# Cross-attention, MLP and a second attention over four batches: entries of the slot tables moved

## The reference

```
z = layer_norm(x, ln1_w, ln1_b)
q = z @ q_w + q_b;  k = ctx @ k_w + k_b;  v = ctx @ v_w + v_b        # 16 heads of 16
o = softmax(q k^T / 4) v                                            # per head
hidden = o @ cproj_w + cproj_b + x
y = gelu(layer_norm(hidden, ln2_w, ln2_b) @ fc_w + fc_b) @ proj_w + proj_b   # 1024 wide
h = hidden + y
# second attention, one head of width 256 over the same context
p = softmax((h @ w_q^T)(ctx @ w_k^T)^T / 16)
out = h + alpha * (p (ctx @ w_v^T)) @ w_o^T
```

## Time and profile before

| | |
|---|---|
| device time, median of 3 runs | 304.48 us (302.76 to 305.58) |
| the profiled execution | 301.47 us, span 299.7 us |
| busy, share of the span | PE 89%, PE weight loads 73%, DVE 70%, ACT 61%, POOL 29% |
| mean granted PE clock | 0.983 of full |
| chain that ended last, by engine | PE 57%, DVE 13%, ACT 9%, POOL 8%, DMA 5%, issue 5% |

### The profile page before, as it was taken

The page is one execution under the profiler, slowest core; times in us unless marked ns, Lnnn a source line. Parts: engine busy times, 40 slices in busy tenths (PEclk is TensorE's granted clock), DMA queues, the critical chain, the costliest instruction groups (busy, mean ns, idle before and its releaser), DMA issues.

```text
span 299.7 us, 5383 instructions
## 1 busy us (share of the span) xinstructions
PE 266.8 (89%) x2054; PEld 219.3 (73%) x2054; DVE 208.4 (70%) x369; ACT 182.8 (61%) x332; POOL 87.6 (29%) x106
## 2 busy tenths in 40 slices
PE   5966979998988998998979998989998999898995
PEld 4754857795666887776967886668876797678974
DVE  6846686577689689856598689654668665457763
ACT  3762666568584777865465959573647598336522
POOL 5360101102022267520031395400031274334000
PEclk9997699999999999999999999999999999999999
DMA  6059948611363330303340420203124000000001
GB/s 219 13 75 185 220 97 266 155 46 36 80 161 71 142 81 0 83 0 111 121 116 7 164 53 30 53 29 88 63 91 142 1 2 0 0 2 0 2 35 35
DMA packets 16424, 23.02 MB, mean 77 GB/s; under 512 B 2512, under 2 KB 9168, under 8 KB 16400
## 3 DMA queue, kind: packets, MB, share of 16 engines
q1 hardware_dynamic: 13088, 16.98, 22.8%
q10 hardware_dynamic: 3312, 5.71, 6.1%
HBM read 12.07 MB, written 1.05 MB: 44 GB/s over the span
## 4 chain that ended last, share of the span: by engine, by line
PE 57%; DVE 13%; ACT 9%; POOL 8%; DMA 5%; issue 5%; SPq 1%; ACTq 1%; POOLq 0%; DVEq 0%
PE work_ps L619 11%; PE om L703 8%; PE s L693 7%; PE s L667 7%; PE work_ps L623 5%; PE work_ps L606 4%; DVE neg_max L1437 4%; DMA q_stack<-qp_l 3%; POOL y_l L1801 2%; ACT probs L1114 2%; PE s L619 2%; POOL ft L1796 2%; PE om L682 2%; DMA vecs<-in_vectors_dram 2%; DVE cT_l L1401 1%
## 5 line engine op out<-in xcount | busy, mean ns | idle before, releaser
L1437 DVE TENSOR_REDUCE neg_max<-s 128x1 f32<-128x512 f32 x128 | 83.9, 684 | 25.8 <-PE s L667 25.3
L1114 ACT ACTIVATE probs<-s 128x512 f32<-128x512 f32 x128 | 75.5, 598 | 30.0 <-PE s L693 29.6
L693 PE MATMUL s<-q_stack,k_stack 128*128 128x256 f32 x256 | 56.5, 304 | 4.0 <-ACT probs L1114 2.1
L667 PE MATMUL s<-k_stack,q_stack 96*128 96x512 f32 x128 | 51.8, 436 | 7.1 <-DVE neg_max L1437 3.6
L693 PEld LDWEIGHTS s<-q_stack,k_stack 128*128 128x128 f32 x256 | 43.9, 197 | 10.9 <-ACT probs L1114 4.1
L667 PEld LDWEIGHTS s<-k_stack,q_stack 96*128 96x128 f32 x128 | 23.7, 198 | 17.8 <-DVE neg_max L1437 8.4
L1752 POOL CAST max_cols<-neg_max 128x8 fp32r<-128x8 f32 x16 | 5.8, 363 | 93.3 <-DVE neg_max L1437 93.3
L703 PE MATMUL om<-probs,vals 128*17 128x256 f32 x512 | 30.7, 380 | 0.0
L703 PEld LDWEIGHTS om<-probs,vals 128*17 128x17 f32 x512 | 13.4, 97 | 11.6 <-issue 0.2
L1106 ACT ACTIVATE q_stack<-om 8x1024 fp32r<-8x1024 f32 x16 | 16.3, 1019 | 7.6 <-PE om L682 7.3
L1128 ACT ACTIVATE y_h<-work_ps 128x512 fp32r<-128x512 f32 x12 | 7.2, 597 | 18.5 <-PE work_ps L623 17.0
(11 more groups left out here) (298 smaller groups left out, 675.0 us busy)
## 6 DMA issues: line engine op xcount, KB each, us to landing
k_stack<-kp_h SPq DMA_DIRECT2D x32, 128.0 KB
cx<-in_ctx_t_dram SPq DMA_DIRECT2D x4, 512.0 KB, 4.5
k_stack<-kp_l SPq DMA_DIRECT2D x16, 128.0 KB
q_stack<-qp_h SPq DMA_DIRECT2D x30, 64.0 KB
pcx<-in_ctx_dram ACTq DMA_DIRECT2D x3, 512.0 KB, 3.4
pT_raw<-in_ctx_t_dram ACTq DMA_DIRECT2D x3, 512.0 KB, 4.4
xz<-in_x_dram SPq DMA_DIRECT2D x5, 256.0 KB, 3.3
raw_late<-in_L_xattn_fc_w_dram SPq DMA_DIRECT2D x1, 1024.0 KB, 6.8
```

What stands on the lines that cost most here:

```text
L667: pe.matmul(s1[:, s1_bank(b, SLOTS * g + s), :], q_stack[0:ROW_MAX, hd, chunk(t)], k_stack[0:ROW_MAX, hd, :], start=True, stop=True).then_ ...
L693: mm = pe.matmul(s2[:, s2_bank(b, SLOTS * g + s), i * LQ:(i + 1) * LQ], k_stack[:, hd, chunk(k)], q_stack[:, hd, :], start=True, stop=True)
L1114: act.activation(probs[:, g % 2, s // 2, k:k + 2, :], s2[:, s2_bank(b, SLOTS * g + s), :].rearrange("p (k n) -> p k n", k=2), ACT.Exp).the ...
L1437: dve.tensor_reduce(neg_max[:, g % 2, s % 2, s // 2:s // 2 + 1], s1[:, s1_bank(b, SLOTS * g + s), :], AX.X, ALU.max, negate=True).then_inc ...
```

## The change

Numbers in the tables move; nothing else. The work and its amount are the same, the order on PE, DVE, ACT and POOL is not. SP's order is the same.

```diff
-POST_FIRST = (8, 11, 12, 13, 14, 15, 19, 25, 26, 31, 35)
+POST_FIRST = (7, 8, 13, 19, 20, 24, 25, 28, 30, 31, 32, 33, 34, 37)
-LN1_APPLY_AT = 8
-CT_AT = {7: 0, 8: 1}
-CT_LOW_AT = {8: 0, 9: 1}
-PRE_AT = {9: 0, 10: 1, 16: 2, 22: 3}
+LN1_APPLY_AT = 9
+CT_AT = {9: 0, 10: 1}
+CT_LOW_AT = {13: 0, 14: 1}
+PRE_AT = {9: 0, 11: 1, 17: 2, 22: 3}
...
-EARLY_AT = {11: 0, 14: 1, 16: 2, 24: 3}
+EARLY_AT = {11: 0, 13: 1, 16: 2, 29: 3}
```

More of the change, by code:

```diff
@@ L69 @@
 FIRST_ORDER = (U_ZT, U_K, U_Q, U_K + 1, U_V, U_V + 1)
-POST_FIRST = (8, 11, 12, 13, 14, 15, 19, 25, 26, 31, 35)
+POST_FIRST = (7, 8, 13, 19, 20, 24, 25, 28, 30, 31, 32, 33, 34, 37)
 LN1_AT = 7
-LN1_APPLY_AT = 8
-CT_AT = {7: 0, 8: 1}
-CT_LOW_AT = {8: 0, 9: 1}
-PRE_AT = {9: 0, 10: 1, 16: 2, 22: 3}
+LN1_APPLY_AT = 9
+CT_AT = {9: 0, 10: 1}
+CT_LOW_AT = {13: 0, 14: 1}
+PRE_AT = {9: 0, 11: 1, 17: 2, 22: 3}
 V_AT = {36: 0, 38: 1}
-POST_AT = {7: 'OT', 8: 'NT', 9: 'CP', 11: 'ZT', 14: 'F0', 15: 'F1', 18: 'F2', 19: 'F3', 20: 'PJ0', 21: 'PJ1',
+POST_AT = {7: 'OT', 8: 'NT', 9: 'CP', 11: 'ZT', 14: 'F0', 16: 'F1', 18: 'F2', 19: 'F3', 20: 'PJ0', 21: 'PJ1',
            22: 'CT0', 24: 'PJ2', 25: 'CT1', 26: 'PJ3', 27: 'CX', 28: 'HT', 29: 'G', 30: 'S0', 31: 'S1', 33: 'PT0',
            34: 'PT1', 35: 'PC', 36: 'DL'}
-EARLY_AT = {11: 0, 14: 1, 16: 2, 24: 3}
+EARLY_AT = {11: 0, 13: 1, 16: 2, 29: 3}
 LATE_AT = {7: 'OT', 9: 'NT', 11: 'CP', 14: 'ZT', 16: 'F0', 20: 'F1', 22: 'F2', 23: 'PJ0', 25: 'F3', 26: 'PJ1',
-           27: 'CT0', 29: 'PJ2', 30: 'CT1', 32: 'PJ3', 34: 'CX', 37: 'HT', 38: 'G', 41: 'S0', 43: 'S1', 46: 'PT0',
-           47: 'PT1', 49: 'PC', 51: 'DL'}
+           28: 'CT0', 29: 'PJ2', 31: 'CT1', 32: 'PJ3', 33: 'CX', 37: 'HT', 38: 'G', 43: 'S0', 44: 'S1', 46: 'PT0',
+           48: 'PT1', 50: 'PC', 51: 'DL'}
 PREP_AT = {12: 'WA', 13: 'WT', 18: 'WO', 20: 'WC', 22: 'CB', 23: 'WF0', 24: 'CB1', 25: 'CB2', 26: 'WF1', 27: 'WP0', 28: 'WP1', 40: 'END'}
-PREP_LOW_AT = {12: 'WA', 13: 'WT', 19: 'WO', 20: 'WC', 25: 'WF0', 26: 'CB', 29: 'WF1', 32: 'WP0', 38: 'WP1'}
+PREP_LOW_AT = {13: 'WA', 15: 'WT', 23: 'WO', 24: 'WC', 26: 'WF0', 27: 'CB', 30: 'WF1', 33: 'WP0', 37: 'WP1'}
 GELU_CUBE, GELU_TANH, GELU_Y, GELU_SPLIT = 1, 2, 3, 4
@@ L111 @@
 PREP_USES = ("WA", "WT", "WO", "CB")
-TAIL_AT = {7: 'WTH', 8: 'WTL', 9: 'C20', 13: 'C21', 18: 'CW0', 24: 'CW1', 25: 'O0 O1', 30: 'N0', 32: 'O2',
-           34: 'O3 CPa N1', 36: 'CPb', 37: 'K4', 39: 'ZT K4', 40: 'F0', 42: 'F1', 43: 'F2', 44: 'F3', 45: 'PJ0',
-           48: 'PJ1 PJ2', 51: 'PJ3', 52: 'HT0', 58: 'HT1', 59: 'S0', 60: 'S1', 63: 'PT0 PT1', 65: 'DL0 DL1'}
+TAIL_AT = {7: 'WTH', 8: 'WTL', 9: 'C20', 13: 'C21', 18: 'CW0', 22: 'CW1', 23: 'O0 O1', 26: 'N0', 31: 'O2',
+           34: 'O3 CPa N1', 36: 'CPb', 37: 'K4', 39: 'ZT K4', 40: 'F0', 42: 'F1', 43: 'F2', 44: 'F3', 46: 'PJ0',
+           50: 'PJ1 PJ2', 51: 'PJ3', 52: 'HT0', 54: 'HT1', 59: 'S0', 60: 'S1', 65: 'PT0 PT1', 68: 'DL0 DL1'}
 LAST_SLOT = 70
```

## The result

The changed kernel takes 307.81 us (median of 17 runs, 306.43 to 310.92), the kernel before in the same comparison 304.48 us (17 runs, 301.79 to 309.21): 1.0151 of it, 95% interval [1.0124, 1.0178]. It is slower, where 302.6 us and a range from 299.2 to 304.9 were forecast. The profiled execution has a span of 305.6 us against 299.7.

A forecast was written before the change was run, and what follows sets the result against it. Time could only go where PE waits, 9.96 us within reach. Terms -1.5 - 1.7 + 0.8 + 0 + 0.5 = -1.9 us, taken off the 304.48 us median, gave 302.6 us, range 299.2 to 304.9.

The forecast's parts named there:

- part 1: Start of iteration 0: maxima come first, so PE's waits of 1.25 and 0.27 us go; -1.5 us.
- Rival (c): New waits before PT0 and between slots 12 and 14 of iterations 1 and 2 drop the clock: 309 us; chance 0.09.
- the side "slower": Whole kernel: a measured time above 307.5 us, more than about 1% slower; chance 0.07.
- The prediction's own sign of being wrong: Wrong if the heads' gains survive slot 14, or the clock drops after slot 7 of iteration 0.
- part 2: End of iteration 0: second key projection, moved from slot 24 to 29, fills PE's waits; -1.7 us.
- part 3: Iterations 1 and 2: heads' gain given back at slot 14, slot 22 slower by 0.4 us each; +0.8 us.
- parts 4 and 5: Iteration 3, slots 22 to 33, taken as 0, and the epilogue, +0.5 us.
- the two waits: Start of iteration 0: PE's 1.25 us for a maximum and 0.27 us for a bank, both forecast to go.
- the third wait: End of iteration 0: PE's 0.31 us at 75.61, tied to POOL's cast at slot 29, forecast to go.
- rival (a): Iterations 1 and 2: DVE and POOL miss each other, heads' gains partly kept; -4.8 us, 299.7 us; chance 0.27.
- rival (b): End of iteration 0: the key projection's fill does nothing, ACT's queue counts; -0.2 us, 304.3 us; chance 0.14.
- Part 5: Epilogue: the 0.98 us wait ahead of PJ0 goes, but PT0 comes 0.5 us later; +0.5 us.

The follow-up runs named there:

- head_alone: The kernel before with only the moves at the head of the iterations, SP order untouched: 309.67 us, ratio 1.0203 to the kernel before.
- load_later: The changed kernel with the `proj_w` load issued on SP after the stacking of batch 1's first group: 298.45 us, ratio 0.9846 to the kernel before.
- before_later: The kernel before with the `proj_w` load moved behind the stacking of batch 1's first group: 303.79 us, ratio 1.0025.
- load_first: The changed kernel with SP waiting for the `proj_w` load to land before issuing the stacking: 308.51 us, ratio 1.0188 to the kernel before.
- key_back_later: `load_later` with batch 1's second key projection back at slot 24 of iteration 0: 300.83 us, ratio 0.9933 to the kernel before.
- gelu_back: `load_later` with F1 back at slot 15 and the first key projection at slot 16 in iterations 1 and 2: 299.36 us, ratio 0.9861.
- ct_late: `load_later` with the context's low parts at slots 14 and 15 instead of 13 and 14: 298.36 us, ratio 0.9850 to the kernel before.
- scores_back: `load_later` with only S0 and S1 of the last iteration's output path back at slots 41 and 43: 298.18 us, ratio 0.9869.
- tail_back: `load_later` with `TAIL_AT` and `LATE_AT` of the kernel before: 299.79 us, ratio 0.9883 to the kernel before.

## Why the prediction was wrong

**The step that failed** is in part 1: "What is late next would be `xz` for its transpose at slot 11, two slots later: covered." Only engines were looked at. SP's stacking of the next batch is released by PE's exp tile of slot 15 and comes sooner with it; the load of `proj_w` ahead of it on SP hangs on nothing in the tables. The kernel before left them 4.7 us apart, so that the key copies were issued when most of the load had moved; the lead that part 1 wins leaves 2.8 us. That two transfers can be issued in the same order and still collide was in none of the terms, and "SP's order is the same" was no answer to it. `head_alone` shows that part 1 suffices, `load_later` and `before_later` that the collision is the whole loss, `load_first` that the two transfers slow each other. Why they do, beyond taking turns, is open. The Trainium skill, "SBUF — State Buffer", section "Door 1: The DMA port swizzle (why `[64,N]` ≈ `[32,N]`)", says that a transfer's rate depends on how many of SBUF's ports its partitions reach; each stacking copy writes 16 rows, and no run here tried another shape.

**Rival (c)** had the second half of the mechanism, a wait and then half clock, but in another place, at 3.3 us a place; here it cost 5.2. It was given 0.09 and the side "slower" 0.07. That its 309 us lie near the measured 307.81 is luck: the sum behind it, two falls of the clock in iterations 1 and 2 or the epilogue, did not happen. Nor does the length of the wait alone decide, as it supposed: PT0's wait of 1.96 us passed at full clock in the changed kernel and in `load_later`. The prediction's own sign of being wrong, a clock that drops after slot 7 of iteration 0, came true.

**The terms without the collision** stand in `load_later`, by the table above (each is the change of its lead over its stretch; 0.16 us of lead are there at slot 7 already):

| | forecast | measured |
|---|---|---|
| part 1, to slot 23 of iteration 0 | -1.5 (-0.9 to -1.9) | -2.49 + 0.16 = -2.3 |
| part 2, to slot 38 | -1.7 (-1.1 to -2.1) | -4.38 + 2.49 = -1.9 |
| part 3, iterations 1 and 2 | +0.8 (-2.1 to +1.4) | -3.53 + 4.38 = +0.85 |
| parts 4 and 5 | +0.5 | -3.1 + 3.53 = +0.4 |
| sum | -1.9 | -2.9 |

Part 1 was put too low: the two waits give 1.5 us, and the rest comes in steps of 0.2 to 0.3 us, at slots 9, 16 and 23 among others, where the rows give no wait, so "time can only go where PE waits" was too narrow. Part 2 is right and is shown twice: `key_back_later` costs 1.41 us, the 0.48 and 0.93 us to the hundredth, and the third wait stays away. Part 3 is right in its size. The heads gain and slot 14 takes it back: between slots 8 and 19 of iteration 1 the lead of `load_later` goes from 4.70 to 5.55 us at slot 14 and back to 4.41 us, through a wait of 1.21 us there (0.5 to 1 was forecast). At slot 22 cubic and `y` both take 1.8 us; `gelu_back` gets back 0.75 us over both iterations, against a forecast of 0.8. The queue of DVE and the wait of POOL share the loss at slot 14: `ct_late` freed the one and met the other. So rival (a) falls, DVE and POOL meet at each of these places, and rival (b) falls by `key_back_later`. Part 5 is right: PT0's wait is 1.96 us (1.3 to 1.7 was forecast), and `scores_back` undoes it for 0.5 us. In the prediction's arithmetic the range's upper end should be 304.8 and not 304.9 us (304.3 and half a us); nothing hangs on it.

The Trainium skill, "SBUF — State Buffer", section "SBUF: two separate sides", says that DVE with two inputs from SBUF and a GpSimd operation take a shared pair of ports in turn, each for a whole instruction. The rows here agree: a cast of 0.58 us beside a low part, and a cubic, an addition and `y` of 1.74 to 1.78 us in a row.

## What to carry to other kernels

A step that PE reaches sooner also starts its DMAs sooner: list each transfer that is released there with what is in flight at the new time and how much room it had, even where the queue's order is unchanged. A transfer that nothing needs for 20 us belongs behind one that PE needs in 10. And a wait costs more than its length when the clock falls after it, here 5.2 us on top of 3.9, so one such wait outweighs half a dozen small gains.

## What the runs showed of the hardware that was not expected

- A 1 MB load that moves 332 GB/s without the stacking, and the stacking's copies within SBUF, 109 GB/s alone, moved 77 GB/s together from 56 to 59 us with the DMA engines 0.82 busy. Issued 5.8 us later, behind the load, the copies were there 1.5 us sooner.
- A shorter wait did not make the loss by the clock smaller: with 2.81 us (`load_first`) as with 3.91 us it was at 0.50 from 62 to 74 us. Counted from slot 7, `load_first` reaches the max tile 1.1 us sooner than the changed kernel and the end only 0.1 us sooner.
- The clock also fell without a wait. In `tail_back` it was 0.58 from 64 to 68 us, with PE busy throughout, right behind 24 products of one column (128x1); in `load_later` the same work kept 1.00. The wait of the changed kernel stands between such products too, and no run here tells how much of its fall is theirs. In `gelu_back` it fell in the epilogue behind a wait of 1.96 us that other kernels passed at full clock. Executions of one kernel differ by 1.5 us (`gelu_back`, mostly 0.977 against 0.983, though one of its long ones has 0.983) to 4 us (`tail_back`, 0.971 against 0.983) along with it, more than most of the edits are worth.
